# GpSimd instead of VectorE raises the rounding constant (a bf16 maximum), with a new order of work

## What is computed

```
x = x + 0.5 * ffn(layernorm(x))      # "A"
x = x + ssm(layernorm(x))            # "S"
x = x + 0.5 * ffn(layernorm(x))      # "C", same weights as A

ffn:  h = silu(q(x) @ q(w_gate).T) * (q(x) @ q(w_up).T);  h = q(h) @ q(w_down).T      (256 -> 704 -> 256)
q(v): for each block of 16 along the last axis
      scale = max(max|v| / 6, 1e-12)
      nearest of 0, .5, 1, 1.5, 2, 3, 4, 6 to |v| / scale, times sign(v) * scale
ssm:  dt = clip(softplus((x @ W_dt1 + b_dt1) @ W_dt2 + b_dt2))
      for each of 16 states: h[t] = exp(A*dt[t]) * h[t-1] + expm1(A*dt)/(A*dt) * dt * B[t] * x[t]
      y = sum over states of h * C[t], + D * x
```

## Time and profile before

| | |
|---|---|
| median of 3 runs | 4263.15 us (4262.46 to 4264.17) |
| profiled execution, whole | 4264.34 us |
| its span | 4262.6 us |
| mean granted TensorE clock | 0.965 |
| busy: PE / DVE / ACT / POOL | 93% / 88% / 77% / 38% |
| maximum on DVE, `magic` (line 660) | 256 instructions, 338 ns mean |
| maximum on DVE, `x_magic` (line 619) | 128 instructions, 360 ns mean |

### The profile page before, as it was taken

One profiled execution on the slowest core, in us unless ns is written; L12 is line 12 of the kernel. 1 busy time (PEld: TensorE's weight loads), 2 busy tenths in 40 slices (PEclk: granted clock), 3 DMA queues, 4 the chain that ended last, 5 costly groups with the idle time before them and its releaser, 6 DMA issues. The chain is left out here.

```text
span 4262.6 us, 73878 instructions
## 1 busy us (share of the span) xinstructions
...
## 2 busy tenths in 40 slices
...
GB/s 28 10 11 16 6 16 11 16 16 16 6 16 11 16 16 16 16 6 15 12 16 16 16 6 16 11 16 16 16 15 8 11 16 16 16 16 6 11 11 10
DMA packets 47540, 57.49 MB, mean 13 GB/s; under 512 B 8583, under 2 KB 42824, under 8 KB 47176
## 3 DMA queue, kind: packets, MB, share of 16 engines
...
...
## 5 line engine op out<-in xcount | busy, mean ns | idle before, releaser
L717 DVE TENSOR_TENSOR_SCAN state<-w_ps,decay 128x512 f32<-128x512 f32 x1024 | 1210.5, 1211 | 28.2 <-PE w_ps L1109 20.7
L1109 PE MATMUL w_ps<-dif,bx 128*128 128x129 f32 (+1 forms) x8192 | 1087.6, 281 | 30.3 <-DVE c_state L710 23.7
L1040 PE MATMUL gu_ps<-wgu,qxT 128*128 128x352 f16 x6144 | 1050.1, 324 | 63.2 <-DVE hid L640 49.9
L1109 PEld LDWEIGHTS w_ps<-dif,bx 128*128 128x128 f32 x8192 | 1017.1, 196 | 110.5 <-issue 91.6
L1040 PEld LDWEIGHTS gu_ps<-wgu,qxT 128*128 128x128 f16 x6144 | 607.6, 101 | 431.6 <-DVE hid L640 73.0
L911 ACT ACTIVATE bx<-s_xh,B_tok 128x256 f32<-128x256 f32 x2048 | 862.1, 498 | 18.0 <-DVE B_tok L678 16.9
L727 DVE SCALAR_TENSOR_TENSOR c_state<-state,inv_A,rep_ps 128x512 f32<-128x512 f32 x1024 | 722.4, 737 | 30.7 <-PE rep_ps L1118 20.4
L1047 PE MATMUL td_ps<-wd,qhT 128*128 128x256 f32 x3072 | 727.5, 387 | 20.1 <-ACT qhT L844 20.1
L421 POOL TENSOR_TENSOR val<-val,magic 128x704 f32<-128x704 f32 x256 | 409.4, 1599 | 886.5 <-DVE magic L660 886.5
L920 ACT ACTIVATE decay<-dt,A_sb 128x512 f32<-128x512 f32 x1024 | 691.1, 714 | 5.0 <-DVE state L717 2.4
L1047 PEld LDWEIGHTS td_ps<-wd,qhT 128*128 128x128 f32 x3072 | 569.9, 192 | 121.1 <-ACT qhT L844 36.8
...
## 6 DMA issues: line engine op xcount, KB each, us to landing
...
b_C<-in_L_attn_b_in SPq DMA_DIRECT2D x5, 0.1 KB
...
```

Of the source, the lines that this page charges most:

```text
L717: v.tensor_tensor_scan(state[:, n % 2, gi, :], w_ps[:, gi, :], decay[:, n % 2, gi, :], 0.0, ALU.add, ALU.mult).then_inc(state_ready.sem, 1)
L1040: last = te.matmul(gu_ps[:, m, 0:FH], qxT[:, t // 2, 4 * (t % 2) + xp * G + c], wgu[:, c, wp, a:a + FH], start=begin, stop=end)
L1109: last = te.matmul(w_ps[:, gi, t * P:t * P + wide], bx[:, n % 2, t, gi * P:(gi + 1) * P], dif[:, 0:wide], start=t == 0, stop=t == T - 1, s ...
```

## The change

GpSimd makes the maximum itself, in `round_x` and `round_h`, in front of its addition, and waits there for ScalarE. VectorE's functions `magic_x` and `magic_h` and their 12 pieces per iteration (`qm`, `xm`) are gone. GpSimd's list is as before. The lists of PE, DVE and ACT hold the same other pieces in a new order. The scan gets one more wait, on the product with C of step m-4, an instruction of VectorE itself that read the buffer which the scan overwrites.

```
             def round_x(q, k):
                 cols = slice(k * (T // 2) * DM, (k + 1) * (T // 2) * DM)
+                pool.wait_ge(x_abs_ready.sem, x_abs_ready.at(q, k + 1))
+                g.tensor_scalar(x_magic[:, cols], x_magic[:, cols], MAGIC, None, ALU.max).then_inc(x_magic_ready.sem, 1)
                 pool.wait_ge(x_magic_ready.sem, x_magic_ready.at(q, k + 1))
...
             def round_h(q, t):
                 s = t % 2
+                pool.wait_ge(abs_ready.sem, abs_ready.at(q, t + 1))
+                g.tensor_scalar(magic[:, s], magic[:, s], MAGIC, None, ALU.max).then_inc(magic_ready.sem, 1)
                 pool.wait_ge(magic_ready.sem, magic_ready.at(q, t + 1))
...
-            def magic_x(q, k):
-                cols = slice(k * TH * DM, (k + 1) * TH * DM)
-                dve.wait_ge(x_abs_ready.sem, x_abs_ready.at(q, k + 1))
-                v.tensor_scalar(x_magic[:, cols], x_magic[:, cols], MAGIC, None,
-                                ALU.max).then_inc(x_magic_ready.sem, 1)
...
-            def magic_h(q, t):
-                dve.wait_ge(abs_ready.sem, abs_ready.at(q, t + 1))
-                v.tensor_scalar(magic[:, t % 2], magic[:, t % 2], MAGIC, None, ALU.max).then_inc(magic_ready.sem, 1)
...
                 dve.wait_ge(decay_ready.sem, decay_ready.at(seq, m + 1))
+                if n >= 2:
+                    dve.wait_ge(c_state_ready.sem, c_state_ready.at(seq, m - G + 1))
                 dve.wait_ge(w_ready.sem, w_ready.at(seq, G + m + 1))
```

The lists, at the places that the text speaks of:

```
 PE, start of S
-    S.z0 S.k0 S.k1 S.w0 A.gu5 S.c0 S.w1 S.e0 S.e1 A.ht0 A.gu6 A.ht1 A.gu7 A.ht2 A.dn0 S.w2 S.w3
+    S.z0 S.k0 S.k1 S.w0 S.w1 A.gu5 S.e0 S.e1 A.ht0 S.c0 A.gu6 A.ht1 A.gu7 A.ht2 S.w2 A.dn0 S.w3
 PE, end of the list
-    S.w29 C.dn2 S.p25 S.w30 C.ht9 S.p26 S.c14 S.p27 C.ht10 S.w31 C.ht11 S.p28 S.c15 C.dn3 N.tx0 S.p29 N.tx1 S.p30 S.p31
+    C.dn2 S.w29 C.ht9 S.w30 C.ht10 S.p26 S.c14 S.p27 C.ht11 S.w31 C.dn3 S.c15 N.tx0 N.tx1 S.p28 S.p29 S.p30 S.p31
 DVE, start of S
-    A.hid3 C.xm0 A.am1 A.qs0 S.cb0 S.sc0 A.qm0 S.k0 S.k1 C.xm1 A.hid4 A.qp0 S.dt0 A.hid5 C.qy0 A.hid6 A.qm1 A.am2 S.g0 S.g1
+    A.hid3 A.am1 A.qs0 S.cb0 S.k0 S.k1 A.hid4 C.qy0 A.qp0 S.sc0 S.dt0 A.hid5 A.am2 A.hid6 S.g0 S.g1
 DVE, end of the list
-    S.p26 C.qp3 N.xm0 C.res2 S.p27 S.g29 S.p28 N.xm1 S.p29 S.g30 S.g31 N.qy0 N.qy1 S.p30 S.p31 C.res3 S.y0
+    C.qp3 S.g27 S.g28 C.res2 S.p26 S.p27 S.g29 S.g30 S.p28 S.p29 N.qy0 N.qy1 S.g31 S.p30 S.p31 C.res3 S.y0
```

More of the change, by code:

```diff
@@ L28 @@
     "PE": """
[L29 to L33, removed]
@@ L34 @@
-    S.p17 C.ht2 S.c10 S.p18 C.dn0 S.w22 S.w23 C.ht3 S.c11 S.p19 S.p20 C.ht4 S.w24 S.w25 C.ht5 S.p21 S.p22 S.c12
-    C.dn1 S.w26 S.w27 C.ht6 S.p23 S.c13 S.p24 C.ht7 S.w28 C.ht8 S.w29 C.dn2 S.p25 S.w30 C.ht9 S.p26 S.c14 S.p27
-    C.ht10 S.w31 C.ht11 S.p28 S.c15 C.dn3 N.tx0 S.p29 N.tx1 S.p30 S.p31
+    A.gu0 A.gu1 A.gu2 S.xt0 A.gu3 S.bt0 S.cm0 S.rb0 A.gu4 S.z0 S.k0 S.k1 S.w0 S.w1 A.gu5 S.e0 S.e1 A.ht0 S.c0
+    A.gu6 A.ht1 A.gu7 A.ht2 S.w2 A.dn0 S.w3 S.p0 S.p1 A.ht3 S.c1 C.tx0 C.tx1 A.ht4 S.w4 S.w5 A.ht5 S.p2 S.p3
@@ new lines @@
+    S.c2 A.dn1 S.w6 S.w7 C.gu0 S.c3 S.w8 S.w9 S.p4 S.p5 S.p6 S.w10 S.p7 A.ht6 S.c4 C.gu1 C.gu2 A.ht7 S.w11 C.gu3
+    S.w12 S.c5 A.ht8 S.p8 S.w13 A.dn2 C.gu4 S.c6 S.p9 S.w14 S.w15 C.gu5 S.c7 S.p10 S.p11 S.p12 A.ht9 S.w16 S.w17
+    C.gu6 S.c8 S.p13 A.ht10 S.p14 S.w18 S.w19 A.ht11 S.c9 S.p15 C.gu7 A.dn3 S.w20 C.ht0 S.w21 C.ht1 S.p16 S.c10
+    S.p17 C.ht2 S.w22 C.dn0 S.c11 S.w23 C.ht3 S.p18 S.p19 S.p20 C.ht4 S.w24 S.w25 C.ht5 S.c12 S.p21 S.p22 C.dn1
+    S.w26 S.w27 C.ht6 S.p23 S.p24 C.ht7 S.w28 C.ht8 S.p25 S.c13 C.dn2 S.w29 C.ht9 S.w30 C.ht10 S.p26 S.c14 S.p27
@@ L37 @@
+    C.ht11 S.w31 C.dn3 S.c15 N.tx0 N.tx1 S.p28 S.p29 S.p30 S.p31
     """,
     "DVE": """
[L39 to L47, removed]
+    S.ln0 A.hid0 C.ln0 A.hid1 A.am0 A.hid2 C.xa0 C.xa1 C.xs0 C.xv0 C.xv1 S.tb0 A.hid3 A.am1 A.qs0 S.cb0 S.k0
@@ new lines @@
+    S.k1 A.hid4 C.qy0 A.qp0 S.sc0 S.dt0 A.hid5 A.am2 A.hid6 S.g0 S.g1 S.p0 S.p1 S.g2 A.hid7 A.qp1 A.res0 C.qy1
+    S.g3 S.p2 S.p3 A.am3 A.qs1 S.g4 S.g5 S.p4 S.p5 A.res1 S.g6 S.g7 S.p6 S.g8 S.p7 A.qp2 S.g9 C.hid0 S.g10
+    C.hid1 S.p8 S.p9 C.am0 C.hid2 S.g11 C.hid3 C.am1 S.p10 S.p11 C.qs0 A.qp3 S.g12 S.g13 A.res2 S.p12 S.p13
+    C.hid4 S.g14 S.g15 C.hid5 S.p14 S.p15 C.am2 S.g16 S.g17 C.qp0 S.p16 S.p17 C.hid6 S.g18 S.g19 S.p18 S.p19
+    C.hid7 C.am3 C.qp1 A.res3 C.qs1 S.g20 S.g21 S.p20 S.p21 N.ln0 C.res0 S.g22 S.g23 S.p22 S.p23 S.g24 S.g25
@@ L48 @@
+    N.xa0 N.xa1 S.p24 C.qp2 S.p25 C.res1 S.g26 N.xs0 N.xv0 N.xv1 C.qp3 S.g27 S.g28 C.res2 S.p26 S.p27 S.g29
+    S.g30 S.p28 S.p29 N.qy0 N.qy1 S.g31 S.p30 S.p31 C.res3 S.y0
     """,
     "ACT": """
-    A.gu0 A.gu1 S.ln0 A.gu2 C.ln0 S.xt0 A.gu3 C.ax0 S.b0 S.b1 S.cm0 S.rb0 A.gu4 C.ax1 A.ah0 S.z0 A.gu5 A.ah1
-    A.ht0 A.gu6 S.d0 A.ht1 S.d1 A.ht2 A.gu7 S.d2 S.d3 S.b2 S.d4 A.ht3 C.tx0 A.ht4 S.b3 A.ht5 S.d5 S.d6 S.d7
-    C.tx1 A.ah2 S.b4 S.b5 S.d8 S.d9 S.d10 S.d11 C.gu0 A.ah3 A.ht6 C.gu1 C.gu2 S.b6 S.b7 C.gu3 A.ht7 S.d12 S.d13
@@ L53 @@
-    A.ht8 S.d14 S.d15 C.gu4 S.b8 C.ah0 C.ah1 C.gu5 S.d16 S.d17 A.ht9 S.d18 S.b9 A.ht10 S.d19 S.d20 C.gu6 A.ht11
-    S.b10 C.gu7 S.d21 S.d22 C.ht0 C.ht1 S.d23 C.ht2 S.b11 S.d24 C.ah2 S.d25 S.b12 C.ht3 N.ln0 C.ht4 C.ht5 C.ah3
-    S.b13 S.d26 S.d27 S.b14 C.ht6 C.ht7 S.d28 C.ht8 S.b15 N.ax0 S.d29 S.d30 N.ax1 C.ht9 C.ht10 S.d31 C.ht11
+    A.gu0 A.gu1 S.ln0 A.gu2 C.ln0 S.xt0 A.gu3 C.ax0 S.b0 S.b1 S.cm0 S.rb0 A.gu4 C.ax1 A.ah0 S.z0 A.gu5 A.ht0
+    A.ah1 A.gu6 S.d0 A.ht1 S.d1 A.ht2 S.d2 A.gu7 S.d3 S.b2 A.ht3 S.b3 A.ht4 S.d4 C.tx0 A.ht5 C.tx1 S.d5 S.d6
```

8 lines of the change are left out of this document (4 added, 4 removed).

## The result

The changed kernel is slower. Its median is 4313.6 us (4311.4 to 4314.8, 4 runs) against 4263.1 us; the ratio is 1.0118, with an interval of 1.0100 to 1.0135. The profiled execution took 4311.35 us, its span is 4309.6 us. The prediction was 4226 us, faster by 0.9%, with a range up to 4270: wrong in sign and outside the range.

What follows compares the result with a forecast made beforehand. TensorE was taken to set the pace. Gains of 0.5 (start of S), 0.6 (end of the list) and 0.1 us (small slips) make 1.2 us for about 31 iterations, 37 us: 4263.2 to 4226 us, range 4190 to 4270.

Steps and rivals of the forecast that it cites:

- The price of the maximum: On GpSimd, 0.72 us for 704 elements and 0.52 for 512; upper bounds 1.53 and 1.16 us.
- The place: Start of S: the rounding chain through GpSimd gives the grid at 2080.4, VectorE reaches qp0 at about 2080.5.
- R1: Rival: a dearer maximum delays hid5 at the start of S; slower above about 1.65 us. Mild form, together with R2: 0.20.
- One for one: At hid5, start of S: lateness beyond the covered 0.4 us passes to TensorE in full.
- R1's strong form: The queue in front of hid5 makes the kernel take above 4272 us; chance 0.12.
- The splitting of C: Start of S: its 3.85 us on VectorE now stand in front of hid5, which starts at 2087.6, covered by 0.4 us.
- w0's wait: Start of S: the 0.67 us wait for direct term k0 goes; gain 0.33 to 0.67 us per iteration, 0.5 taken.
- The end of the list: Near the iteration's end: C.res2 comes about 4 us earlier, C.ht9's 0.54 us wait goes; 0.6 us with refill.
- a refill: Near the iteration's end, behind C.ht9's wait: another 0.1 us gained per iteration.
- VectorE's room: VectorE gets back at most 4.1 us per iteration, about 3.5 with overlap; this is room, not time.
- The own wait: The scan's added wait is on an instruction at least four scans back, always done; it costs nothing.
- R2: Rival: shared SBUF access slows small VectorE instructions beside GpSimd; about no change, 4257 us. Chance 0.20 together with mild R1.

Runs made afterwards that it cites:

- e3: The changed kernel with the maximum over only 224 of 704 and 160 of 512 elements, part of the rounding left out: 4238.0 us.
- e9: The changed kernel with one of its 12 maxima, stage A tile 0, back on VectorE between S.cb0 and S.k0: 4248.5 us.
- e10: As e9, with the scan g27 ahead of C.qp3 instead of behind it: 4230.0 us.
- e4: The kernel before the change with only the scan's wait on its own engine added: 4263.0 us.
- e5: The changed kernel with C.qy0 moved back behind A.hid5 in VectorE's list, nothing else: 4305.4 us.

## Why the prediction was wrong

- **The price of the maximum: the step that failed.** The prediction took it between "one operand" and "two tensor inputs", at 0.72 us for 704 elements, and believed the two-input sum, 1.53 us, an upper bound, since the maximum reads less. It takes 1.97 us (median), more than the sum, and e3 shows that 76 us hang on it. The three lengths (766 ns for 224, 1524 for 528, 1966 for 704) lie near a line of 0.2 us and 2.5 ns per element. The memset of the earlier trace rows is a different operation and a write without a read; nothing in the trace bounded the price from above.
- **The place was right.** I wrote that at the start of S the chain "fits, with nothing to spare", and R1 had the mechanism, the place and a deciding price, 1.65 us. With 1.97 us its formula gives 1.73 x 1.97 - 1.25 - 0.4 - 1.2 = 0.56 us per iteration; the middle lost 1.14. "One for one" is not what the trace shows: 19 iterations lost 0.3 us each and ten lost 2.7. R1's strong form had only 0.12, because the price had too narrow a spread.
- **The splitting of C: mis-sized, the other way.** Its 3.85 us held a first step of 1.59 us beside GpSimd's product, at 2073.71 to 2076.44. Behind the grid it took 2.7 us in all. Without this hid5 would have come 1.1 us later still.
- **w0's wait: right.** It is gone. VectorE stands 2.85 us before k0, and that was the place where one maximum was free (e9).
- **The end of the list: half right.** C.ht9's wait fell from 0.54 to 0.25 us. No run shows the 0.1 us of the sum for a refill behind it; they show the wait alone, 0.25 us here and 0.76 in e10. The prediction had not looked at g27, which the new list puts behind C.qp3. In the changed kernel, where qh took 1.27 instead of 0.88 us beside a maximum at that place, w29 waited 0.64 us for it; in e3 no such wait shows.
- **VectorE's room:** of the 4.1 us of maxima per iteration VectorE's busy time fell by 0.8 in the changed kernel, since other instructions grew; in e3 it fell by 3.2, and the iteration by 1.0.
- **The ends: overlooked.** The prediction had no term for them and gave no reason. In the last C alone, with no other work, the rounding chain lies open. GpSimd's timeline, before and then after:

```profile
4222.15 1.52 POOL L421 TENSOR_TENSOR val<-val,magic 128x704 f32<-128x704 f32 x1 [0.28 <-DVE magic L660]
```
```profile
4265.07 1.97 POOL L422 TENSOR_SCALAR magic<-magic 128x704 bf16<-128x704 bf16 x1
4267.12 1.52 POOL L424 TENSOR_TENSOR val<-val,magic 128x704 f32<-128x704 f32 x1
```

  Before, GpSimd stood 0.28 us between the product and the sum; after, the sum starts 2.05 us behind the product. The ends cost 14.1 us in all, 2.1 with the short maximum (e3): 12 us are the price again.
- **The own wait: right**, nothing (e4).
- **Shared access (R2): its longer instructions are there, and larger than the prediction had them; that access is the cause was not shown.** In the kernel before the scale takes 0.47 us at 2071.86, beside GpSimd's sum of x (1.16 us from 2071.11), and 0.205 us mostly. The prediction had 0.8 us of longer VectorE instructions per iteration. The x scale, the `qx` and `qh` products, the scale of hid and the last step of dt grew by 3.3 us together, against the 4.0 that the maxima had taken, and qy0's instruction takes up to 1.75 us instead of 0.41. What that costs is known at one place only: e5 finds 8 us at qy0. e9 took away this stretching together with the late grid, so it does not separate the two.
- **The clock: taken as fixed.** The slow stretch of the earlier trace rows, at 0.50, begins at 2077.9 and by the window with 0.64 ends at 2084.7, so 6.8 us. The prediction let only w0's gain depend on it. It mostly hides where VectorE's queue is the bound, and shows where it doesn't: 2.4 us between the two kinds of iteration. Its length changed from kernel to kernel (6.8 us per iteration in the changed one, 3.4 in e3), and most of what the experiments gained in the middle is that. What decides when it falls was not settled.
